# The two loads of a pair's x, issued from ScalarE's queue instead of SP's

## The reference

```python
x = x + _L0_cond_ref(x, cond[:, None, :], ...)   # attention, each batch element by itself
x = x + _L1_cond_ref(x, cond, 1, 1)              # samples x at positions given by cond
x = x + _L2_cond_ref(cond, x, ...)               # a GRU cell over the 64 time steps
x = x + _L3_cond_ref(cond, cond, x, ...)         # an oscillator, Runge-Kutta, over the same steps

def _L0_cond_ref(x, emb, W_emb, b_emb, g_norm, W_qkv, g_q, g_k, W_out):
    ...
    xn = _rms_norm(x, g_norm) * (1.0 + scale) + shift
    qkv = xn @ W_qkv
    ...
    q = _rms_norm(q, g_q)
    k = _rms_norm(k, g_k)
    logits = jnp.einsum('bhqd,bhkd->bhqk', q, k) * d ** (-0.5)
    attn = jax.nn.softmax(logits, axis=-1)
    o = jnp.einsum('bhqk,bhkd->bhqd', attn, v)
    ...
    return o + o @ W_out
```

## Time and profile before

| what | value |
|---|---|
| median of 3 runs | 1513.64 us |
| lowest, highest | 1509.73, 1516.41 us |
| the profiled execution's own time | 1517.27 us |
| its span in the trace | 1515.2 us |
| mean granted clock of TensorE, as a share of full speed | 0.988 |
| busy in the span: PE, DVE, ACT, POOL | 96%, 84%, 60%, 51% |

### The profile page before, as it was taken

One profiled execution on the slowest core, in us unless ns is written; L12 is line 12 of the kernel. 1 busy time (PEld: TensorE's weight loads), 2 busy tenths in 40 slices (PEclk: granted clock), 3 DMA queues, 4 the chain that ended last, 5 costly groups with the idle time before them and its releaser, 6 DMA issues.

```text
span 1515.2 us, 94439 instructions
## 1 busy us (share of the span) xinstructions
PE 1453.9 (96%) x41966; PEld 1279.7 (84%) x41966; DVE 1275.0 (84%) x3095; ACT 902.3 (60%) x2753; POOL 768.6 (51%) x916
## 2 busy tenths in 40 slices
PE   4799999999999999999999999999999999999997
PEld 2366766666766669999999999999999999999996
DVE  6888888778888776788888889889888888888887
ACT  5567766757767743555555555555555555555553
POOL 2567777757677756443444344344444434434432
PEclk8899999999999999999999999999999999999999
DMA  7477777767777772000000000000000000000000
GB/s 258 82 158 167 162 154 161 166 146 169 170 171 176 153 163 79 12 11 15 15 12 15 15 12 15 15 12 15 16 15 11 15 15 12 15 15 12 15 15 14
DMA packets 188216, 108.74 MB, mean 72 GB/s; under 512 B 134272, under 2 KB 165184, under 8 KB 187808
## 3 DMA queue, kind: packets, MB, share of 16 engines
q1 hardware_dynamic: 187360, 102.45, 28.7%
q10 hardware_dynamic: 448, 0.25, 0.1%
HBM read 50.65 MB, written 11.67 MB: 41 GB/s over the span
## 4 chain that ended last, share of the span: by engine, by line
PE 79%; DVE 9%; DMA 4%; issue 3%; SPq 2%; ACT 1%; POOL 1%; DVEq 0%; ACTq 0%; POOLq 0%
PE psB L1463 35%; PE psA L1492 15%; PE psQ L1174 10%; PE psA L1497 8%; PE psQ L1220 4%; PE psO L1266 3%; DMA first<-qn 2%; DMA PT<-front 2%; PE psO L1254 2%; PE psB L1202 1%; DVE psA L830 1%; SPq L325 1%; DVE qn L770 1%; DVE room L801 1%; DVE oT L893 1%
## 5 line engine op out<-in xcount | busy, mean ns | idle before, releaser
L1463 PE MATMUL psB<-first,Wx 128*128 128x64 f16 x9216 | 290.7, 193 | 1.8 <-issue 1.3
L1492 PE MATMUL psA<-ts,Cp 128*128 128x64 f16 x8160 | 281.0, 193 | 7.1 <-ACT ts L1563 6.4
L1463 PE MATMUL psB<-first,Whh 128*128 128x64 f16 x9072 | 286.2, 193 | 0.8 <-POOL first L1928 0.5
L1174 PE MATMUL psQ<-Wx,front 128*128 128x512 f16 x1152 | 280.1, 391 | 5.5 <-DVE front L982 4.6
L1463 PEld LDWEIGHTS psB<-first,Wx 128*128 128x128 f16 x9216 | 278.0, 98 | 2.8 <-issue 2.4
L1463 PEld LDWEIGHTS psB<-first,Whh 128*128 128x128 f16 x9072 | 273.7, 98 | 1.4 <-POOL first L1928 0.6
L1492 PEld LDWEIGHTS psA<-ts,Cp 128*128 128x128 f16 x8160 | 256.3, 98 | 8.3 <-ACT ts L1563 7.2
L1563 ACT ACTIVATE ts<-qst 128x256 f16<-128x256 f32 x192 | 80.1, 417 | 298.0 <-DVE qst L1676 298.0
L1174 PEld LDWEIGHTS psQ<-Wx,front 128*128 128x128 f16 x1152 | 107.5, 100 | 124.3 <-issue 12.3
L1928 POOL TENSOR_TENSOR en<-rz,dn 128x256 f32<-128x256 f32 x64 | 46.7, 730 | 259.5 <-issue 256.8
L1497 PE MATMUL psA<-ts,Cp 128*128 128x64 f16 x4080 | 161.2, 193 | 0.0
(11 more groups left out here) (199 smaller groups left out, 2899.8 us busy)
## 6 DMA issues: line engine op xcount, KB each, us to landing
rows<-rows_dram SPq DMA_DIRECT2D x64, 256.0 KB, 4.3
front<-in_x SPq DMA_DIRECT2D x32, 256.0 KB, 4.3
XR<-in_x_turned SPq DMA_DIRECT2D x32, 256.0 KB, 4.8
out<-ob SPq DMA_DIRECT2D x63, 128.0 KB, 1.8
x<-x SPq DMA_DIRECT2D x29, 224.0 KB
Whh<-in_W_qkv SPq DMA_DIRECT2D x12, 256.0 KB, 8.3
room<-in_W_hh SPq DMA_DIRECT2D x12, 256.0 KB, 2.7
room<-in_W_ih SPq DMA_DIRECT2D x12, 256.0 KB, 2.9
```

Source lines behind the costliest of these rows:

```text
L1174: last = mm(psQ[:, n, :], xn[p.u][:, i, c, :], Wqkv[:, j, c, n * D:(n + 1) * D], start=(c == 0 and t == 0), stop=(c == KC - 1 and t == 2))
L1463: last = mm(o, W_[:, i, c, g * PART:(g + 1) * PART], src[:, j, c, :], start=False, stop=False, skip_group_check=True)
L1492: mm(psF[:, s % 2, m, :], Cp[:, i, c, m * PART:(m + 1) * PART], ts_[:, 0, c, :], start=(c == 0 and m == 0 and i == 0), stop=False, skip_gr ...
```

## The change

`load_x(p)` moves from SP's program to ScalarE's. In slots 0 to 28 ScalarE issues both transfers behind `squares_qk(pair(0), 0)`, in slot 0 behind the guess as well, ahead of `high_x1`. The loads of pairs 0 to 2, ahead of the loop, stay on SP, and so does every other transfer.

```diff
--- before.py
+++ after.py
@@ -346,8 +346,6 @@
                 turn_p(p, 1)
             if p := pair(-3):
                 load_rows(p, 1)
-            if p := pair(3):
-                load_x(p)
             if i == 2:
                 sp.wait_ge(rows_ready, 1)
                 sp.dma_start(rows_dram.rearrange("b c n -> b (c n)"), i0h.rearrange("b c n -> b (c n)")).then_inc(rows_out, 16)
@@ -542,6 +540,11 @@
             need(act, ssx_done, p.n)
             a(sq[:, 1, :], xtok[p.u][:, :], ACT.Square, scale=X_SCALE, accum_out=ss[:, X]).then_inc(ssx_done, 1)
 
+        def load_x(p):
+            act.wait_ge(rs_T, p.n - 1)
+            act.dma_start(xtok[p.u][:, :], x[bass.ds(p.n * 2, 2), :, :].rearrange("b t d -> (b t) d")).then_inc(x_in[p.u], 16)
+            act.dma_start(of_pair(p).rearrange("p c b t -> p c (b t)"), x_turned[p.n, :, :, :]).then_inc(xr_in[p.n % 4], 16)
+
         def high_qk(p, n):
             act.wait_ge(qn_done if n else q_gained, p.n * 2 + 2 if n else p.n + 1)
             need(act, qk_in, p.n * 32)
@@ -660,6 +663,8 @@
                 if p := pair(2):
                     squares_x(p)
                 squares_qk(pair(0), 0)
+            if p := pair(3):
+                load_x(p)
             if i == 2:
                 high_cp(3)
             if p := pair(-3):
```

## The result

The changed kernel takes 1528.62 us (median of 5 runs, 1522.55 to 1533.89) against 1513.89 us (5 runs, 1509.73 to 1516.41) before: 14.7 us more, a ratio of 1.0099 with a 95% interval of 1.0064 to 1.0134. The forecast was 1519.4, +5.8 us, with the range up to 1532. The measured time lies in the range but beyond 1523, the end of the likeliest case's own range.

What follows compares the result with a forecast made beforehand. TensorE, busy 96% of the span, was taken to bound the kernel; 0 (SP) + 2.2 (late slots) + 0.7 (slot 1) + 2.9 (long issues) + 0 (side by side) = 5.8 us gave 1519.4 us, range 1511 to 1532.

Steps and rivals of the forecast that it cites:

- the likeliest case: Small delays at slots of the pair loop that are already late, +1 to +9 us; own range 1514 to 1523; chance 0.38.
- Off SP: SP's queue in the pair loop: issuing 1.06 us less per slot only makes SP wait longer; value 0.
- ScalarE's issue time: Behind the squares of q: issues of 1.06 us, 0.50 hidden, delay high_x1 by 0.56 us; the minima wait absorbs 0.23.
- What the delay costs: At the q/k and P transposes: 0.2 us of delay costs 2.2 us in late slots, plus 0.7 us in slot 1.
- The 2.2 us (late slots): In the 11 slots where TensorE already waits for landings, 0.2 us of delay each costs in full.
- 0.7 us (slot 1): At the loop's start, the issue pair of 1.06 us less a 0.40 us wait delays the guess in slot 1.
- The long issues, 2.9 us: Issues of x about 1.1 us over median, in 9 of 24 slots, would stop ScalarE's exponentials; half of 5.9 us taken.
- Transfers side by side: x, from another queue about 1.8 us earlier, may overlap P's last packets; bounds 0 to 17.6 us, taken as 0.
- Case 4: P's transposes share the DMA engines with x in the pair loop: +11.7 us, 1525; chance 0.17.
- Case 3: ScalarE stalls in full at the issues, not overlapping the squares, and long issues hit too: +17.5 us, 1531; chance 0.23.
- Signs named in advance: Profile after: TensorE's landing waits 4.7 to 7 to 12 us; VectorE's wait for squares of k 1.19 to about 1.5.

Runs made afterwards that it cites:

- the tiny transfers: The kernel before, x's loads still on SP, plus two 8-byte-piece transfers into an unused tile issued by ScalarE at the changed place: 1517.79 us, 1.0026.
- experiment 10: The changed kernel with x's two loads issued on ScalarE behind the weight piece, ahead of the first exponentials: 1509.09 us, 1.0001 against the kernel before.
- 7: The kernel before, x's loads on SP, plus one ScalarE copy into an unused tile at the changed place in slots 1 to 28: 1515.16 us, 1.0005.
- 2: The changed kernel with x's two loads issued on ScalarE ahead of the squares of q: 1538.93 us, 1.0157 against the kernel before.

## Why the prediction was partly right, step by step

**Off SP: right.** No gain. SP's wait for VectorE before the q/k transposes rose from 120.6 us to 144.9 us in 31 slots, and that for low_x1 from 64.3 to 106.8 us in 27, that is by 0.8 and 1.6 us each, where about 1 was forecast:

```profile
SPq L325 <- DVE qn L775: 144.9, 31, 20.1
SPq L304 <- POOL x L458: 106.8, 27, 5.1
```

**ScalarE's issue time: the mechanism right, the size near.** The issues start in the same instant as the squares of q (220.81) and are hidden behind them for 0.5 us; high_x1 starts 1.05 us behind the squares instead of 0.50, a delay of 0.55 us (0.56 forecast). The wait for the minima took up a part, as forecast.

**What the delay costs: mis-sized.** The 2.2 us (late slots) and 0.7 us (slot 1) are not seen: 0.5 us of ScalarE's time and no transfer gives 1.0005, though a loss of 3 us lies inside the interval.

**The long issues, 2.9 us: wrong in its reason.** They were fewer on ACT: 4 of XR's 24 were over a microsecond, of up to 1897 ns, and none of x's (389 at most). And a ScalarE delayed by 1.6 us in all 28 slots costs only 5.7 us, so 1.1 us in four slots is worth a fraction of one. Whose congestion it was, which the prediction left open, the DMA views show. The 9 long loads before and these 4 all have an instruction packet (q8) that starts between 0.6 us before the issue and its end. One of them is the 1.79 us of the earlier trace rows, from 265.36 to 267.15. Of the 83 shorter issues of x's loads 10 have one. So the long issues go with the instruction queue's packets, in ACT's queue as in SP's; why they are fewer there is open.

**The step that failed: "Transfers side by side ... I take 0, as the likely overlap is the last tenths of P's packets".** This term, with an upper bound of 17.6 us, held most of the 14.7 us: some 11 if the 4 us of the tiny transfers are ScalarE's time. With x's issue moved by one microsecond (experiment 10) the loss goes, with ScalarE delayed alone (7) it does not come, and with ScalarE free and x earlier (2) it grows. I sized the overlap from one ordinary slot, where x goes out 2.8 us behind P and it is indeed harmless, and took that for all. The loss sits in the slots in which P's issue is late, and in these the distance shrinks to 1.2 to 2.1 us, because x is no longer held behind P by a common queue. Case 4, at 0.17, was what happened; its 11.7 us, 1525, is 3 us below the measured time. Case 3, nearer by its number (1531), was not: ScalarE's stall was tested by itself and is small. The 1528.62 lies in the range because case 3 had set the range's end; that was luck, for the mechanism behind the sum's 5.8 us was not the one that acted.

**The rule beside case 4** of the Trainium skill (DMA: Bandwidth & Descriptors, "Queues, rings and completion order"), that each DMA engine takes turns between the queues it has work for: the trace agrees in that both queues move in the same stretch (744 and 125 packets from 223.4 to 224.4). But in the half microsecond from 222.4 SP's queue moved 15 packets and ACT's 65, and why it stood so nearly still was not found.

**Signs named in advance.** TensorE's waits for landings rose to 12.0 us, the upper end of the 7 to 12 given. VectorE's wait for the squares of k did not grow as forecast: its waits for ScalarE's two squares fell together from 44.6 us in 52 times to 31.8 us in 50, for a reason that is open. P's time to land stands in no row of the changed kernel; the time from P's issue to the mix, 6.8 to 8.1 us in the late slots against 5.4 to 6.3, stands in its place, and bears out case 4's sign there.

**Why P is late now and then.** Before and after alike, from 105 to 545 us, 27 pairs of transposes took over 2.8 us to issue. All 27 have an instruction packet that starts between 0.6 us before the issue and its end, against 10 of the 77 pairs that took less. In the slot above it is one that stands in the 3.79 us of the q/k transposes, from 215.75 to 219.54:

```profile
q8 instruction: 1, 0.02, 2.1%
```

So the late slots go with instruction packets that meet an issue; nothing was changed to test it.

**Still open.** How much of a late slot's wait is an instruction packet's, and why SP's queue nearly stands in one slot and is only slowed in others. And what the 4 us of the tiny transfers are: their interval and that of one copy overlap, so they may be 640 small packets beside P or nothing more than ScalarE's time.

## What to carry to other kernels

A load issued behind a transfer that an engine waits for was held back here by the common queue, also in the passes in which that transfer was late; in another queue it was not, and it hurt just there. So before a load moves to another queue, look at the slots in which the critical transfer is issued late, not at an ordinary one, and measure the distance between the two issues in each. If the load must move, put it later in the other engine's program, and measure each place: one microsecond of distance was worth 1% here, and a place later still, behind high_o, cost 1.4%.

## What the runs showed of the hardware

ScalarE's queue issues a transfer while ScalarE computes: the first issue starts with the squares of q, and 0.5 of the 0.93 us is hidden. With 256 KB loads in ACT's queue, the packets of a transpose in SP's fell to 15 in half a microsecond in one slot (228 in the half before) and to 120 in a microsecond in another (624 at the same place without them), and the consumer came up to 2.9 us late. All 40 long issues of the two kernels from 105 to 545 us (pairs of transposes over 2.8 us, loads of x over 1 us), in either queue, had an instruction packet beside them. ScalarE, at 1.6 us more in each slot, cost 5.7 us over 28 slots: an engine with 60% busy time forgave nearly all at this place.
